# Value packs of a causal sixteen-head attention stage, spread over five slots of 256 columns instead of four of uneven width

## The reference

```
Q, K, V = x @ Wq + bq, x @ Wk + bk, x @ Wv + bv     # Q and K then turned by position
scores  = where(key > query, -inf, Q @ K.T)         # per head, 512 x 512
attn    = softmax(scores / sqrt(8))
out     = concat_heads(attn @ V) @ Wo + bo
```

## Time and profile before

| | us |
|---|---|
| median of three runs | 7058.65 |
| lowest and highest | 7045.03, 7066.15 |
| the profiled execution | 7059.09 |
| its span in the trace | 7056.9 |
| PE busy in the span | 5707.9 |
| DVE, ACT, POOL busy | 3650.5, 3275.9, 2346.1 |

### The profile page before, as it was taken

How to read it: one execution, slowest core, us unless ns; L and a number is a source line. 1 busy time by engine, 2 the same in 40 slices (tenths; PEclk the granted TensorE clock), 3 DMA queues, 4 the chain that set the end, 5 groups by cost and what they waited for, 6 DMA issues and landing times. The chain is left out here.

```text
span 7056.9 us, 120786 instructions
## 1 busy us (share of the span) xinstructions
PE 5707.9 (81%) x38044; PEld 2737.2 (39%) x38044; DVE 3650.5 (52%) x5825; ACT 3275.9 (46%) x7054; POOL 2346.1 (33%) x2035
## 2 busy tenths in 40 slices
PE   6998698788769999879999867212488996799999
PEld 2444243333336566446666333201122222344444
DVE  5777323666556665356665444812498883222222
ACT  2666433455636555336566233100177784244333
POOL 3232101222058787158786000464522211000000
PEclk7999899799979999989999988555599997899999
DMA  2433111333200000000000000002133330100000
GB/s 90 109 101 102 31 48 37 105 92 93 61 18 8 6 8 3 4 17 7 5 7 3 4 2 0 14 23 69 37 85 89 85 79 11 64 36 36 36 36 36
DMA packets 279342, 298.80 MB, mean 42 GB/s; under 512 B 80038, under 2 KB 213058, under 8 KB 275778
## 3 DMA queue, kind: packets, MB, share of 16 engines
q1 hardware_dynamic: 266050, 286.19, 14.8%
q0 software_dynamic: 8192, 3.89, 0.3%
q10 hardware_dynamic: 4608, 2.10, 0.1%
HBM read 186.45 MB, written 107.74 MB: 42 GB/s over the span
## 5 line engine op out<-in xcount | busy, mean ns | idle before, releaser
L716 ACT ACTIVATE a_prob<-a_PB 128x512 f32<-128x512 f32 x2304 | 1252.0, 596 | 543.0 <-PE a_PB L592 400.3
L1068 ACT ACTIVATE f_hid<-f_ph,f_bias 128x512 f32<-128x512 f32 x768 | 527.4, 687 | 784.8 <-PE f_ph L1036 782.5
L640 PE MATMUL a_PO<-a_prob,a_V 128*32 128x256 f32 (+3 forms) x8192 | 726.7, 428 | 20.1 <-ACT a_cn L689 19.8
L1036 PE MATMUL f_ph<-H,f_w 128*128 (+1 forms) x1536 | 695.5, 596 | 51.2 <-DMA f_bias<-in_f_b 32.4
L1043 PE MATMUL f_po<-f_hid,f_w 128*128 128x512 f32 x1536 | 690.2, 592 | 0.0
L824 DVE TENSOR_REDUCE a_blocks<-a_PA 128x8 f32<-128x1024 f32 x512 | 608.7, 1215 | 139.6 <-PE a_PA L592 139.2
L827 DVE TENSOR_REDUCE a_neg<-a_PA 128x2 f32<-128x1024 f32 x512 | 592.0, 1215 | 64.2 <-PE a_PA L605 64.2
L605 PE MATMUL a_PA<-a_KS,a_QS 48*128 48x512 bf16 (+3 forms) x3072 | 477.2, 350 | 161.8 <-issue 44.9
L622 PE MATMUL a_PB<-a_QS,a_KS 51*128 51x512 bf16 (+3 forms) x3072 | 453.5, 332 | 81.6 <-ACT a_prob L716 41.4
L2035 DVE TENSOR_REDUCE f1a_neg<-f1a_PA 128x2 f32<-128x384 f32 (+1 forms) x512 | 267.3, 522 | 474.5 <-PE f1a_PA L1837 462.1
L1965 POOL TENSOR_TENSOR f1a_prob<-f1a_prob,f1a_inv 128x384 f32<-128x384 f32 (+1 forms) x512 | 394.6, 773 | 313.8 <-DVE f1a_inv L2039 313.7
(11 more groups left out here) (375 smaller groups left out, 9623.5 us busy)
## 6 DMA issues: line engine op xcount, KB each, us to landing
a_spill<-a_qkp SPq DMA_DIRECT2D x576, 128.0 KB, 2.4
a_QS<-a_spill SPq DMA_DIRECT2D x384, 96.0 KB, 2.6
a_KS<-a_spill SPq DMA_DIRECT2D x384, 96.0 KB, 2.6
f_wt<-token_gates SPq DMA_DIRECT2D x16, 2048.0 KB, 7.2
a_raw<-a_cn SPq DMA_DIRECT2D x192, 72.0 KB
a_heads<-a_raw SPq DMA_DIRECT2D x32, 256.0 KB, 3.3
a_rs<-a_inverses SPq DMA_DIRECT2D x32, 256.0 KB, 3.4
f_w<-in_f_w1e SPq DMA_DIRECT2D x32, 256.0 KB, 2.8
```

The costliest lines, as they stand in the source:

```text
L640: mm = nc.tensor.matmul(PO[32 * j:32 * j + 32, first:last], V[:, par, t, 8 * e + pr], prob[:, k % st.ring, e, c + first - q0:c + last - q0 ...
L716: nc.scalar.activation(prob[:, k % st.ring, e], PB[:, ring_b.slot(0, ("b", s, e))], ACT.Exp, scale=scale).then_inc(pb_used, 1)
L1036: nc.tensor.matmul(ph[:, k], w1[:, u, k * P:(k + 1) * P], H[:, b], start=True, stop=True).then_inc(fc.sem, 1)
L1068: nc.scalar.activation(hid[:, slot, k], ph[:, k], ACT.Gelu_apprx_tanh, bias=bias[:, u, k:k + 1]).then_inc(act_done.sem, 1)
```

## The change

The first pack (512 columns) and the second (384) are issued in two pieces. A pack's last number is its `half`: 0 the queries below 256, 1 those from 256 on, 2 all. `pv_pack` knew the three kinds already; the stage that isn't causal uses the first two. The five slots now hold: t=0 below 256; t=0 from 256; t=1 below 256 (128 columns) and the whole of t=3 (128 columns); t=1 from 256; t=2 (256 columns). The last pack and the evacuation move from slot at+7 to at+8, which for the last group of a batch is slot 9 of the step. The columns multiplied are the same, the packs of a group six instead of four.

```
             if causal:
...
-                self.packs += [(g, 0, at + 1, at + 4, 2), (g, 1, at + 3, at + 5, 2), (g, 3, at + 3, at + 6, 2), (g, 2, at + 4, at + 7, 2)]
-                self.evacuate[g] = at + 7
+                self.packs += [(g, 0, at + 1, at + 4, 0), (g, 0, at + 1, at + 5, 1), (g, 1, at + 3, at + 6, 0), (g, 3, at + 3, at + 6, 2),
+                               (g, 1, at + 3, at + 7, 1), (g, 2, at + 4, at + 8, 2)]
+                self.evacuate[g] = at + 8
```

## The result

The changed kernel takes 7121.28 us (median of four runs, 7113.37 to 7134.90) against 7059.17 of the kernel before on the same chip: 62 us or 0.9% slower, ratio 1.0093 [1.0069, 1.0116]. The profiled execution has a span of 7125.2 us against 7056.9, 68.3 us more, and a mean granted clock of 0.883 against 0.888.

The account below looks back on a forecast made before the run. PE sets the pace, with slot 15 hanging on the last evacuation's chain. Late evacuation + 70, outside slots 8 to 15 - 6, first and last steps + 4, clock + 12: + 80 on 7059.1, 7139 us (7120 to 7158, chance 0.62).

Parts of the forecast that it names:

- the main mechanism: Causal stages: slot 15 hangs on a batch's last evacuation through stores, denominators' fetch and reciprocal, without slack; 70 us for both.
- The last evacuation, the term that counts: Moves from slot 8 to 9, 2.5 us later; 14 steps a stage, 35 us each, 70 for both.
- What lies outside slots 8 to 15: Pack costs and bank wait less removed waits: about - 0.45 us where PE binds, in half of 28 steps, - 6.
- Slot 6 bound by SP: SP's list shifts with the evacuation; where the next step's slot 6 waits for maxima rows, the step grows 2.5 us.
- The clock: Lower clock behind PE's longer waits, 1.5 us a drop, in some 8 more steps: + 12 us, bounds 0 and 42.
- Packs: Four slots of 0.57 us and one with two 128-column packs, near streaming alone; 0.2 to 0.4 us a group, 0.25 taken.
- The bank: Next group's first pack waits for the evacuation of the single accumulator bank: 0.3 to 0.4 us without a Q projection between.
- Everything else of the program unchanged: Sign: only the two causal stages lengthen, steps by 2 to 2.5 us; wrong if another stage changes its length.
- A: Rival: the clock falls in every step of the causal stages, + 80 + 30, 7169 us; chance 0.18.
- B: Rival: the evacuation chain has unseen slack, only pack costs and bank wait remain, about + 5, 7064 us; chance 0.05.
- C: Rival: evenness pays, waits on ACT and DVE go, second 128-column pack free; - 25, 7034 us; chance 0.03.
- D: Rival: the shift counts in one path only, say half of the steps absorb it; + 40, 7099 us; chance 0.12.

Follow-up runs that it names:

- E1: Kernel before, with only the last group's evacuation of each batch moved a slot later, packs as before; 7123.58 us, ratio 1.0106 to the kernel before.
- E2: Changed kernel, but the last of a batch's four groups keeps the old packs and its evacuation in slot 8; 7052.63 us, ratio 0.9998 to the kernel before.
- E5: Kernel before, first two packs each cut in two in their old slots, evacuation unmoved, as many PE instructions as the changed kernel; 7060.20 us, ratio 1.0018.
- E3: Changed kernel with DVE's reciprocal two slots later, in slot 15 instead of 13; 7124.86 us, ratio 1.0104 to the kernel before.
- E12: Kernel before with 32 repeated tiny matmuls in the first phase, so later PE code lies 128 instructions further on; 7073.16 us, ratio 1.0006.
- E10: E2 with the same three order edits as E9; 7040.82 us, ratio 0.9980 to the kernel before.
- E9: Kernel before with denominators fetched ahead of four loads, maxima rows ahead of group 2's loads, reciprocal in slot 14; 7039.26 us, ratio 0.9987.
- E6: Kernel before with 64 repeated tiny matmuls in the first phase, so later PE code lies 256 instructions further on; 7076.26 us, ratio 1.0037.
- E15: Changed kernel with DVE's reciprocal in slot 15 and the maxima rows' DMAs issued by POOL instead of SP; 7033.73 us, ratio 0.9955 to the kernel before.

## Why the prediction came out as it did

It was right on the main mechanism and on its place, and 18 us high against the median (7139, measured 7121.28); on the profiled span it said + 80 and + 68.3 was measured. Point by point:

- *The last evacuation, the term that counts.* Forecast 2.5 us later, measured 2.50; slot 8 to slot 15 forecast 15.0 us, measured 15.05 and 15.52 in the mean; the growth of that half step 2.39 and 2.38 us, forecast 2.5 and 2.4. The reciprocal came 8.7 to 10.3 us after the evacuation (said: 8.8 to 10), slot 15 1.69 to 1.78 after it, DVE idle 3.6 to 5.8 (said: 3 to 5), PE idle about 2 in the first stage and 2.4 to 4.1 in the second (said: 2, and 2 to 4). E1 and E2 show that this is the cause.
- *What lies outside slots 8 to 15.* Forecast - 0.45 where PE binds (the terms written there give - 0.40) and 0 where SP does. Measured - 0.37 and - 1.40. In the first stage's 12 stretches PE was idle 10.7 us less, lost 13.6 more to the clock and did 7.3 less work, which had moved ahead of slot 15. In the second stage 9.9 us of second pauses fell away, 0.8 a step, which no step of the working had. With it that stage grew by 14.5 us where 35 were forecast; against E5, which has the same code places, by 29.9.
- *Slot 6 bound by SP.* Said: SP's list shifts with the evacuation, so that a step whose slot 6 hangs on SP grows by the full 2.5 us; its wait there would then stay. The wait shrank, from 9.4 to 4.9 us and from 18.1 to 11.3 us in the second stage: slots 15 to 18 lost 39.8 us to the clock (before 5.0) and the bank waits came on top, and so PE came later to slot 6. This step of the working was wrong and cost little, because the wait at slot 15 had already put its 2.5 us into the step. E3 shows that SP's end was close behind: with slot 15 free, slot 6 took over 14.1 us in the first stage and 45.4 in the second.
- *The clock.* Counted in 8 more steps at 1.5 us, + 12. It is 19 more (22 of 26 against 3), and 1.5 x 19 = 28 us; the table has 27.3 us more lost to the clock. So the sum had this term too small by more than half. The time did not come out longer for it, since a part of the loss is taken back at slot 6, where PE comes later and waits less: the stretches from slot 15 to slot 8 lost 23.4 us more to the clock and were still 21.3 us shorter. That the sum is not too low in spite of this term is luck. The Trainium skill (TensorE: Matmul & The Clock Gate, HAM oscillation) warns that a kernel which idles between bursts in every round starts each round slow, and the trace agrees in 22 of 26 rounds.
- *Packs.* Forecast 0.57 and two of 128 near streaming alone. Measured 0.58 for the two (572.63 to 573.21), where one takes 0.36: the second costs 0.22. The rule of the Trainium skill that only a change of mode drains (TensorEngine Tiling (Array Packing), Key Properties) holds here.
- *The bank.* Forecast 0.3 to 0.4 us for each such wait; measured 11.2 us in 30, 0.37 each.
- *"Everything else of the program unchanged."* Wrong, and by the prediction's own list a sign of being wrong: + 12.3, + 19.9 and - 13.6 us in stages that the change doesn't touch. E5 and E12 show the code's place as the cause. In E5, which has the code places without the late evacuation, the causal stages are 21.5 us shorter than before and these three 20.8 longer, and so the sum came close partly because these cancel. Against E5 the change cost 67.0 us in the causal stages, where 80 were forecast.
- *The rivals.* A (every step pays the clock) was nearly right in the count of steps (22 of 26), not in the sum. B and C fell with E1 and E2, and C's premise that evenness pays 25 us finds no support in E10 against E9 (equal within 0.1%). D, half of the steps absorb the shift, fell: no step had slack (the shortest of the 26 takes 14.75 us from slot 8 to 15, the shortest before took 12.49).

A length of one stage from one trace is known less well than the tables look: the first causal stage, untouched by E6 and E12, is 709.5 us before and 703.1 and 706.2 there. Differences under some 6 us are not explained here.

## What to carry to other kernels

Before work is evened out on the engine that sets the pace, follow the last result of a round through the queues to the next thing that this engine waits for; if that chain has no slack, moving its start by a slot costs that slot in each round, whatever the evened work gives. A chain that an engine meets at two places must be loosened at both: here one alone gave nothing and the two together 1.4% of the changed kernel's time. When a wait and the lower clock behind it are gone from one place, look for both at another before the clock is ruled out. And compare a kernel whose program got longer with one of the same length that does the old work, since stages that are not touched can move by more than the change does.

## What the runs showed of the hardware

- Behind the end of a loop turn PE can pause twice: 2.7 to 4.5 us at the turn in the causal stages and 2.1 to 3.8 in the local attentions, and 0.6 to 3.2 us again some 3 us later, or not; which it is moved with the place of the code. A shift of 128 instructions moved these pauses between stages (E12), one of 256 left them (E6). Single stages changed by up to 26 us; over the whole run these largely cancelled (E5, 0.18% in all).
- A fetch of data just stored has to wait until the stores have landed: 5.93 to 6.00 us from the first of the four stores' issue to that of the fetch, with four loads between them or without (E9). The four loads cost nothing at that place.
- PE's idle time of 1.8 to 4.1 us ahead of slot 15 was followed in 22 of 26 steps by a stretch at 1.2 GHz, which cost 39.8 us in slots 15 to 18, 1.8 a step; before the change, with 0 to 2.2 us of idle time there, it was 3 of 26. In E3, where the idle time moved to slot 6, the lower clock moved behind it.
- The lower clock took 48 us of the 976 us in the 26 steps before and 75 us of 1017 after; it fell to 20 of 906 in E15, where most of the waits were gone.
